# Three-stage transformer block with experts: kept sums inverted tile by tile, another order of copies, picks and router, and the third expert and gate of one more unit behind the loop

## The reference, cut to what matters

```
x = x + self_attn(ln(x)*(1+sc_msa)+sh_msa) * g_msa          # windows of 128, 16 heads of 16
h = ln(x)*(1+sc_mca)+sh_mca                                   # cross attention to 77 rows
scores = einsum('bqhd,bkhd->bhqk', q, k) / sqrt(D)
top_s, top_i = top_k(scores, 16); attn = softmax(top_s)
x = x + (einsum('bhqk,bhqkd->bqhd', attn, v at top_i) @ w_co + b_co) * g_mca
x = x + swiglu(ln(x)*(1+sc_mlp)+sh_mlp) * g_mlp
# second layer
nx = layer_norm(x); weights = softmax((nx@Wq) @ (bank@Wk).T / 16); evidence = weights @ (bank@Wv)
combined = concat(nx, evidence, anchor); router_probs = softmax(combined @ router_W + router_b)
h = silu(einsum('btc,ecr->bter', combined, e_w1) + e_b1)      # 3 experts, 512 wide
routed = sum((h @ e_w2 + e_b2) * router_probs)
g = sigmoid(silu(combined @ gate_w1 + gate_b1) @ gate_w2 + gate_b2)
out = x + g * (routed @ out_w + out_b)
```

## Time and profile before

| | |
|---|---|
| median of 3 runs | 1443.78 us (1443.26 to 1445.39) |
| profiled execution | 1448.53 us, of which the span of the trace is 1446.7 us |
| PE busy | 1404.7 us, 97% |
| PEld, DVE, ACT, POOL busy | 81%, 74%, 57%, 30% |
| granted TensorE clock, mean | 0.99 |
| chain that ended last | PE 73%, DVE 21%, issue 3% |

### The profile page before, as it was taken

The page is one execution under the profiler, slowest core; times in us unless marked ns, Lnnn a source line. Parts: engine busy times, 40 slices in busy tenths (PEclk is TensorE's granted clock), DMA queues, the critical chain, the costliest instruction groups (busy, mean ns, idle before and its releaser), DMA issues.

```text
span 1446.7 us, 29891 instructions
## 1 busy us (share of the span) xinstructions
PE 1404.7 (97%) x9585; PEld 1177.1 (81%) x9585; DVE 1066.6 (74%) x4754; ACT 818.8 (57%) x2523; POOL 440.5 (30%) x600
## 2 busy tenths in 40 slices
PE   6999999999999999999999999999999999998997
PEld 5778788888888788888888788888888878887886
DVE  3485868788796878879697777869688786968632
ACT  2473374747556384665747466574757547474433
POOL 1314132323315232331335132232334313232302
PEclk9999999999999999999999999999999999999999
DMA  7520000010010000010010000000010000000000
GB/s 244 178 93 2 1 2 25 2 34 9 19 33 13 4 2 25 1 34 1 23 36 1 16 1 16 11 20 16 9 35 17 16 2 7 3 1 9 1 2 14
DMA packets 32760, 35.29 MB, mean 24 GB/s; under 512 B 8744, under 2 KB 27868, under 8 KB 32349
## 3 DMA queue, kind: packets, MB, share of 16 engines
q1 hardware_dynamic: 32605, 33.38, 7.6%
HBM read 28.83 MB, written 4.22 MB: 23 GB/s over the span
## 4 chain that ended last, share of the span: by engine, by line
PE 73%; DVE 21%; issue 3%; ACT 1%; POOL 1%; SPq 0%; DMA 0%; DVEq 0%; POOLq 0%; ACTq 0%
PE bank L964 16%; PE bank L1033 11%; PE bank L973 8%; PE bank L1009 7%; DVE knocked L2266 7%; PE bank L824 6%; PE bank L1016 4%; PE bank L873 4%; DVE M L2259 3%; PE bank L810 2%; PE bank L863 2%; DVE M L2254 2%; PE bank L885 2%; PE bank L781 2%; PE bank L924 2%
## 5 line engine op out<-in xcount | busy, mean ns | idle before, releaser
L964 PE MATMUL bank<-hB,Wm 128*128 128x256 f32 x1024 | 244.0, 385 | 2.5 <-ACT hB L1404 2.5
L964 PEld LDWEIGHTS bank<-hB,Wm 128*128 128x128 f32 x1024 | 191.8, 191 | 34.2 <-issue 7.0
L1009 PE MATMUL bank<-nxT,W1nx 128*128 128x256 f32 x896 | 212.6, 383 | 0.0
L1443 ACT ACTIVATE prob<-bank,rmax 128x128 f32<-128x128 f32 x512 | 180.8, 433 | 29.6 <-DVE rmax L2193 29.6
L1801 POOL TENSOR_TENSOR scores<-scores,M 128x308 f32<-128x308 f32 x128 | 94.8, 741 | 315.3 <-DVE knocked L2266 313.1
L1033 PE MATMUL bank<-W2p,gT 128*128 128x256 f32 x768 | 183.2, 381 | 3.0 <-DVE acc L2345 1.9
L1009 PEld LDWEIGHTS bank<-nxT,W1nx 128*128 128x128 f32 x896 | 166.5, 191 | 23.3 <-issue 2.8
L1033 PEld LDWEIGHTS bank<-W2p,gT 128*128 128x128 f32 x768 | 141.2, 190 | 23.8 <-issue 2.8
L1493 ACT ACTIVATE tbs<-bank,b1half 128x256 f32<-128x256 f32 x128 | 60.8, 475 | 144.6 <-PE bank L964 140.6
L1509 ACT ACTIVATE tbs<-bank,betaH 128x256 f32<-128x256 f32 x224 | 96.1, 493 | 80.2 <-PE bank L1016 79.0
L1443 ACT ACTIVATION_READ_ACCUMULATOR prob<-bank,rmax 128x1 f32 x512 | 139.7, 273 | 0.0
(11 more groups left out here) (240 smaller groups left out, 2817.6 us busy)
## 6 DMA issues: line engine op xcount, KB each, us to landing
Wm_g<-in_L_xcond_w_m_dram SPq DMA_DIRECT2D x4, 1024.0 KB, 5.4
W1ev<-in_L_xcond_e_w_dram SPq DMA_DIRECT2D x6, 512.0 KB, 7.4
x<-in_x_dram SPq DMA_DIRECT2D x16, 128.0 KB, 2.7
x<-in_x_dram SPq DMA_DIRECT2D x32, 64.0 KB, 2.3
Wm<-in_L_xcond_w_m_dram SPq DMA_DIRECT2D x1, 2048.0 KB, 9.8
out_dram<-acc SPq DMA_DIRECT2D x16, 128.0 KB, 1.7
out_dram<-acc SPq DMA_DIRECT2D x32, 64.0 KB, 2.0
batch_rows<-row_store SPq DMA_DIRECT2D x4, 384.0 KB, 3.9
```

Of the source, the lines that this page charges most:

```text
L964: m = pe.matmul(bank_of(name)[:, half * UT:(half + 1) * UT], Wm1[:, k, c:c + P], hB[:, k, :], start=(k == 0), stop=(k == CB - 1))
L1009: pe.matmul(bank_of(name)[:, n * UT:(n + 1) * UT], W1nx[:, k, c0 + n * P:c0 + (n + 1) * P], nxT[:, k, :], start=(n == 0 and k == 0), stop= ...
L1443: m = act.activation(prob[:, s, i, :], psum[s][:, i * P:(i + 1) * P], ACT.Exp, bias=rmax[:, t, s * HPS + i:s * HPS + i + 1], accum_out=rsu ...
```

## The change

1. The kept sums are inverted and spread by tile: DVE has `a_invert_kept(t)` twice, POOL `a_spread_kept(t)` twice, and PE waits for each tile's half of r2.
2. Order in each turn (and in last_cross): DVE does `a_bias_queries` three calls earlier, `a_pick(1, 0)` one earlier, and sum and inverse of tile 0 ahead of the last `a_topk`. ACT does `a_copy_picked(0, 3)` ahead of `b_proto_exp`, and both `a_kept_exp` ahead of the first expert's tanh. PE does `a_v(1)` ahead of `a_turn_picked(0, 2)`, and `b_router` ahead of r2's turn.
3. The third expert and the gate of unit 13 (NU-3), with their mix and finish, move from the last loop turn into `last_cross`; the MLP of unit 14 then uses the tile `prob` for its hidden layer.
4. In last_cross and last_experts `b_first_nx("h21")` stands ahead of `b_second(1, (0, 1))`.

```diff
-    for _p in (NU - 1, NU):
+    for _p in (NU - 2, NU - 1, NU):
...
         def gated_of(u):
-            return gT_last if isinstance(u, int) and u >= NU - 1 else gT
+            return gT_last if isinstance(u, int) and u >= NU - 2 else gT
...
# PE, a_turn_inverses
-                for f in range(CB):
-                    for t in range(1 if values == "pv" and u >= 2 else TILES):
+                for t in range(1 if values == "pv" and u >= 2 else TILES):
+                    if values == "xv":
+                        pe.wait_ge(spread_x, u * TILES + (t + 1))
+                    for f in range(CB):
...
# PE, both
                 b_turn_normed(b)
+                a_v(1, a)
                 a_turn_picked(0, 2, c)
...
                 a_turn_picked(0, 3, c)
-                a_v(1, a)
...
+                b_router(b)
                 a_turn_inverses("r2", "xv", c)
-                b_router(b)
...
-                b_second(2, (0, 1), b)
+                if b < NU - 3:
+                    b_second(2, (0, 1), b)
                 turn("ln3", xnB, c, normed[2], TILES)
...
# PE, last_cross
                 a_turn_picked(0, 0, c)
+                b_second(2, (0, 1), b - 1)
+                b_second(2, (2, 3), b - 1)
+                b_gate(b - 1)
                 b_turn_normed(b)
...
                 b_second(0, (2, 3), b)
+                b_first_nx("h21", 2 * RH + 2 * P, b)
                 b_second(1, (0, 1), b)
-                b_first_nx("h21", 2 * RH + 2 * P, b)
...
# ACT, both
                 a_cross_exp(1, 1, c)
-                a_kept_exp(0, c)
...
+                a_kept_exp(1, c)
                 b_tanh_first("h00", hE[:, 0], 0, 0, b)
-                a_kept_exp(1, c)
...
# POOL
+            def a_spread_kept(t, u):
+
+                pool.wait_ge(kept_inverted, u * TILES + (t + 1))
+                pool.tensor_copy(kept[:, t], kinv[:, t, :].rearrange("p (h a) -> p h a", a=1).to_broadcast([P, H, D])).then_inc(spread_x, 1)
...
+                a_spread_kept(0, c)
                 a_shift_kept(1, c)
-                a_spread("xv", c)
+                a_spread_kept(1, c)
...
# DVE, last_cross
                 a_pick(0, 1, c)
+                b_mix(2, b - 1)
...
                 a_pick(1, 1, c)
-                a_sum_kept(0, c)
+                b_finish(b - 1, xs[(b - 1) % UNITS])
                 a_sum_kept(1, c)
```

More of the change, by code:

```diff
@@ L97 @@
             for _job in _late:
-                if _p == NU and DEFERRED[_job] == _name:
+                if _p > NU - 2 and DEFERRED[_job] == _name:
                     TAIL_ORDER[_job, _p - 2] = _n
@@ L1485, in b_tanh_mlp @@
                 if j == 0:
-                    if isinstance(u, int) and u >= NU - 1:
+                    if isinstance(u, int) and u >= NU - 2:
                         act.wait_ge(gated, u * len(FIRST_ORDER))
@@ L1502, in b_tanh_first @@
                     wait_drained(act, f"m{HJ - 2 + i}", u)
[L1503 removed]
+                if i == 0 and isinstance(u, int) and u >= NU - 2:
                     wait_full(act, "e2", u - 1)
[L1505 removed]
+                if i == 1 and isinstance(u, int) and u >= NU - 2:
                     act.wait_ge(mixed, u + 1)
@@ L1656, in both @@
                 a_copy_picked(0, 2, c)
+                a_copy_picked(0, 3, c)
                 b_proto_exp(b)
                 a_cross_exp(1, 0, c)
-                a_copy_picked(0, 3, c)
+                a_kept_exp(0, c)
                 a_copy_values(a)
@@ L1812, in a_spread @@
             def a_spread(values, u):
[L1814 to L1819, removed]
-                alone(pool)
-                for t in range(1 if values == "pv" and u >= 2 else TILES):
-                    i = pool.tensor_copy(each[values][:, t], inv[:, t, :].rearrange("p (h a) -> p h a", a=1).to_broadcast([P, H, D]))
-                i.then_inc(spread if values == "pv" else spread_x, 1)
+                pool.wait_ge(sums_inverted, u + 1)
+                alone(pool)
+                for t in range(1 if u >= 2 else TILES):
+                    i = pool.tensor_copy(each[values][:, t], rinv[:, t, :].rearrange("p (h a) -> p h a", a=1).to_broadcast([P, H, D]))
+                i.then_inc(spread, 1)
+            def a_spread_kept(t, u):
+                pool.wait_ge(kept_inverted, u * TILES + (t + 1))
+                pool.tensor_copy(kept[:, t], kinv[:, t, :].rearrange("p (h a) -> p h a", a=1).to_broadcast([P, H, D])).then_inc(spread_x, 1)
             def gate(w, n, b, done):
@@ L2537, in both @@
                 b_proto_norm(b)
+                a_bias_queries(a)
                 a_topk("a", 1, 3, c)
+                a_pick(1, 0, c)
                 a_topk("b", 1, 2, c)
+                a_sum_kept(0, c)
+                a_invert_kept(0, c)
                 a_topk("b", 1, 3, c)
-                a_pick(1, 0, c)
-                a_bias_queries(a)
                 a_pick(1, 1, c)
-                a_sum_kept(0, c)
                 a_sum_kept(1, c)
-                a_invert_kept(c)
+                a_invert_kept(1, c)
                 b_silu("h00", hE[:, 0], 0, b)
```

44 lines of the change are left out of this document (27 added, 17 removed).

## The result

The changed kernel takes 1491.24 us (median of 4 runs, 1489.77 to 1492.42); the ratio to before is 1.0319, with a 95% interval of 1.0304 to 1.0334. It is 3.2% slower. The forecast was 1444.0 us and the range 1438.0 to 1448.5, so the prediction was wrong by 47 us. Two further runs of the kernel before, 2895.49 us here and 5058.34 us beside the experiments, stand far off all others and are left out of the ratios; no trace shows what disturbed them.

What follows compares the result with a forecast made beforehand. DVE's list from the residual to the reciprocal was taken to bound each loop turn, PE only following. Terms +2.1 (loop) + 0.6 - 0.1 - 2.4 = +0.2 us, with the runs' median 4.75 below the profile, gave 1444.0 us, range 1438.0 to 1448.5.

Steps and rivals of the forecast that it cites:

- DVE's order: Loop: tile 0's sum and reciprocal delay tile 1's second pick by 0.62 us; the 0.60 saved at r2 is lost earlier.
- ACT's walk: Loop, second path: last MAX8 2.11 us later, h00 behind the kept exponential, y10's copy holding the router until 1100.05.
- ACT becomes the releaser: Slower rival, loop: POOL's shift 0.3 us later delays y10's copy, 14 x 0.45 = 6.3 us, 1448.2 us; chance 0.18.
- 1.8 us after one empty stretch: Last query turn: half clock after idling slows the queries, turning a gain of 1.2 us into a loss of 0.6.
- Per-tile inverses: Loop, r2: only tile 1's half stays late, so the 0.60 us wait goes; 14 x 0.60 = 8.4 us at stake.
- the router in front: Loop, ahead of r2: helps remove r2's wait; router and r2 cost what they did, 0.44 and 0.49 us.
- a_v(1) ahead: Loop, ahead of `a_turn_picked(0, 2)`: covers a wait of 0.3 us a turn, but costed at nothing since DVE sets the stretch.
- The faster rival: Loop: picks not delayed the full 0.62, each turn gains 0.3 to 0.6 us, 1433.5 to 1437.7 us; chance 0.22.
- The tail: Behind the loop: +0.6 at the query turn, -0.1 in last_cross, -2.4 for h21; -1.9 us in all.
- the deferral: Third expert and gate of unit 13 moved to last_cross: +0.6 us at the query turn, -0.1 in last_cross.
- h21: Two last turns: h21 moved ahead of the second expert product covers PE's wait for a shared bank, 2 x -1.2 = -2.4 us.

Runs made afterwards that it cites:

- the version of 1433.60 us: Changed kernel with DVE's pick, sum and inverse behind the last MAX8, POOL's shift before spread, ACT's exponential behind h00, a_v(1) behind the picks: 1433.60 us, ratio 0.9924.
- the run of 1543.11 us: Changed kernel with DVE's first pick of tile 1 and tile 0's sum and inverse back behind the last MAX8, ACT's new order kept: 1543.11 us, ratio 1.0685.

## Why the prediction was wrong

**The step that failed** stands under "DVE's order": "That pick releases `a_turn_picked(1, 2)`, and that stands ahead of everything." It took the pick for the only releaser. The turn has two, the scores and its bank, and the second is bank 2, whose sequence has h00 in front of y12. The trace of before could not show this, since a wait names only what came last, and h00 was drained 1.4 us early. The table of banks showed it. For bank 0 I had followed the very same link (y10's copy ahead of the router's product), for bank 2 not.

**ACT's walk itself held.** It had h00 drained at 1099.45, 20.25 us behind DVE's residual at 1079.20; measured is 1132.20 behind 1111.72, 20.48, and 20.16 in the turn before. The link alone was missing: with it the six transposes would have gone from 1098.4 to some 1099.6, and the sum from +0.15 to about +1.35 a turn (an estimate from the prediction's own walk), 19 us in 14 turns and a forecast near 1461 us. Measured with the clock kept up: +1.21 a turn and 1459.87 us. And where the link is harmless because ACT's line is put back, the loop costs +0.17 a turn: the path over DVE was sized rightly.

**The rival "ACT becomes the releaser"** named the right engine and the right idle stretch, but hung on y10's copy, and so was priced at 0.45 a turn. The engine was found; the job behind it on the list that PE needs first was not.

**The clock was priced in the tail only.** The prediction gave it 1.8 us after one empty stretch, and not one for 14 waits, because it had no wait over 0.7 us in the loop. The runs have 31 us for it. The Trainium skill (TensorE: Matmul & The Clock Gate, section What's actually happening), with its throttled default and the clock released by activity, agrees in direction: idle products alone brought the mean from 0.971 to 0.994.

**"Per-tile inverses" and the router in front**: r2's wait did go in all 14 turns, and this is worth 0.31 us a turn where nothing else is moved. I had it at stake for 0.60 and given back whole.

**"DVE's order"**: the pick was to come 0.62 later. The rows of before have 17.71 us from the residual to the second pick (1079.20 to 1096.91), the changed kernel 18.82 (1111.72 to 1130.54), 1.11 more. But turn 13 is one of the shortest of before and one of the longest of the changed kernel. Over the loop's 14 turns this stretch takes 17.71 to 18.06 us before, 17.85 in the mean, and 18.49 to 18.90, 18.59 in the mean, after: 0.74 more, near the 0.62. So the turns do not repeat each other to 0.1 us here, as the prediction has it, and one turn can't carry a difference of this size. The run with ACT's line put back shows what this costs on its own: 1.09 us of wait at the pick, where 0.6 to 0.7 was forecast, in place of 0.44 at r2.

**"a_v(1) ahead"**, costed at nothing, was right: the wait only shows up at pw instead.

**The faster rival** did not come true in the changed kernel. The Trainium skill (Perfetto Trace Analysis, section Optimizing Scalar/DVE Operations), named beside it, has it that breaking up instructions may let work complete sooner. The split itself does no harm, as the version of 1433.60 us has it; what it gains alone was not run. What came with it did harm. To have tile 0 ready early, DVE's list got work ahead of the last MAX8, on which POOL's shift waits; ACT's list got the waiting exponential of tile 1 ahead of h00's ready tanh; and POOL's list got a waiting spread ahead of the shift, which cost nothing in the changed kernel, but in the run of 1543.11 us, where the inverse came late, PE's wait in turn 13 was 3.70 us, against 0.62 with spread and shift swapped.

**The tail** came out as forecast in the profiles, 138.9 us from the so-projection to the last L1036 (1342.38 to 1481.26) against 140.8, -1.9. This agreement is luck. The kernel before with only ACT's line moved has 137.7 there (1297.80 to 1435.50): the 3 us between these two profiles go with the clock of the execution (from 1340 to 1345 it was 0.77 in that of before, in the other 1.00). Of the parts, the deferral gains nothing that can be measured, and h21 perhaps 1 to 2 us.

## What to carry to other kernels

Before an instruction is moved, list for each instruction that may come to wait on it all that it waits for: the data, and whoever empties the buffer it writes. Read the order of the buffers' jobs, since the profile shows the latest releaser alone. An instruction that waits for a late producer must not stand on an in-order engine ahead of ready work that another engine needs; look at each list it passes, POOL's too. A repeated idle stretch of TensorE is to be priced with the clock behind it, which here was twice the price of the wait; where it can't be removed, products that nobody reads fill it, if they are shorter than the wait.

## What was not expected of the hardware

The wait alone does not decide whether the clock falls: behind 2.17 us of idling the clock stayed at 1.00 in one turn and behind 2.16 us it was 0.55 over the next 7.6 us. What tells the two apart stays open. Where the wait was 3.70 us (the run of 1543.11 us), the stretch behind it was all at the lower level:

```profile
1080.20:1088.00 7.80, 7.80 (x62) 6.48 (x66) 1.76 (x5) 4.16 (x11) 0.00 (x0) 0.50 0.00 0
```

The kernel before has no fixed time. Of its 23 runs beside the last four kernels, the eight with a mean granted clock of 0.994 took 1440.35 to 1440.99 us, the nine with 0.990 took 1447.51 to 1448.72, and the others lie between in the same order. The 8 us from the fastest to the slowest go with the clock; a gain of 2 us shows in many runs and in their clocks, never in two profiles. The turns of the loop are steadier: 1090.4 to 1090.7 us over 13 in the profiles of the kernel before and of the three with its loop or with ACT's line alone moved, whose mean clocks lie from 0.990 to 0.992.
